# Grouping attention's matmuls by kind on TensorE, and layer norm in two bunches on VectorE

## The reference, cut to what matters

```python
h = _layernorm(x) * (1 + ca) + sa                       # modulation per sequence
x1 = _layernorm(h, ln1_g, ln1_b)
Q, K, V = low-rank projections of x1 (16 heads of 8)
scores = einsum('bhse,bhte->bhst', Q, K) / sqrt(8)      # causal mask
attn = softmax(scores, axis=-1)
ctx = einsum('bhst,bhtd->bhsd', attn, V)
h = h + ctx @ out_U @ out_V + out_b                     # then MLP, router, experts
```

## Time and profile before

| | |
|---|---|
| median of 3 runs | 906.88 us (906.5 to 907.08) |
| the profiled execution's own time | 905.57 us |
| its span, first to last instruction | 902.9 us |
| attention | from the start to about 447 us of the span |
| steady steps of attention | about 95 to 411 us |
| TensorE busy over the whole span | 672.0 us (74%) |
| VectorE, ScalarE, GpSimd busy | 419.0, 419.8, 312.9 us |

### The profile page before, as it was taken

One profiled execution on the slowest core, in us unless ns is written; L12 is line 12 of the kernel. 1 busy time (PEld: TensorE's weight loads), 2 busy tenths in 40 slices (PEclk: granted clock), 3 DMA queues, 4 the chain that ended last, 5 costly groups with the idle time before them and its releaser, 6 DMA issues. The chain is left out here.

```text
span 902.9 us, 15792 instructions
## 1 busy us (share of the span) xinstructions
PE 672.0 (74%) x5322; PEld 407.9 (45%) x5322; DVE 419.0 (46%) x1079; ACT 419.8 (46%) x733; POOL 312.9 (35%) x491
## 2 busy tenths in 40 slices
PE   4447999989899999998178885753328799999900
PEld 3213334433334433432146554433026699899900
DVE  1568887777775666661148763800003011111117
ACT  5120666656666665558255654311012355555513
POOL 2441323323332222121134432277730154455523
PEclk9999999999999999999679996985559799999965
DMA  8233323333333333112294111011100677778627
GB/s 178 83 111 128 110 81 127 99 111 106 122 100 125 105 124 106 47 48 76 67 271 92 46 47 61 30 55 51 51 27 0 184 226 215 223 208 227 187 87 207
DMA packets 104347, 102.68 MB, mean 114 GB/s; under 512 B 12912, under 2 KB 88600, under 8 KB 104192
## 3 DMA queue, kind: packets, MB, share of 16 engines
q1 hardware_dynamic: 95264, 89.12, 33.4%
q0 software_dynamic: 4544, 9.45, 3.0%
q10 hardware_dynamic: 4480, 3.35, 1.5%
HBM read 58.97 MB, written 38.72 MB: 108 GB/s over the span
## 5 line engine op out<-in xcount | busy, mean ns | idle before, releaser
L962 DVE TENSOR_REDUCE row_max<-ps_s 128x1 f32<-128x384 f32 (+3 forms) x384 | 216.2, 596 | 98.9 <-PE ps_s L722 75.8
L583 ACT ACTIVATE work<-ps_s 128x1024 f32<-128x1024 f32 (+1 forms) x192 | 168.5, 883 | 67.2 <-PE ps_s L751 64.7
L722 PE MATMUL ps_s<-k_st,q_st 128*128 128x384 bf16 (+3 forms) x512 | 129.2, 309 | 0.0
L1531 POOL DMA_INDIRECT y_d<-res,target x78 | 74.9, 960 | 124.5 <-DVE res L1596 109.5
L719 PE MATMUL ps_s<-later_q,ident_b 128*128 128x128 bf16 (+1 forms) x384 | 94.4, 250 | 17.2 <-DVE row_max L962 13.8
L768 PE MATMUL ps_pv<-work,v_sb 128*32 128x512 f32 (+3 forms) x1024 | 95.5, 446 | 1.3 <-ACT ctx_raw L617 1.2
L719 PEld LDWEIGHTS ps_s<-later_q,ident_b 128*128 128x128 bf16 x384 | 37.2, 98 | 113.2 <-DVE row_max L962 78.9
L1596 DVE TENSOR_TENSOR res<-ps_s,bias 128x256 f32<-128x256 f32 x39 | 16.6, 425 | 137.1 <-PE ps_s L1583 134.2
L1583 PEld LDWEIGHTS ps_s<-w_tile,x_hidden 128*128 128x128 f32 x624 | 75.6, 192 | 2.0
L1573 PE MATMUL ps_s<-tok_t,w_tile 128*128 128x256 f32 x312 | 76.2, 388 | 0.0
L1583 PE MATMUL ps_s<-w_tile,x_hidden 128*128 128x128 f32 x624 | 75.8, 275 | 0.0
(11 more groups left out here) (198 smaller groups left out, 1028.4 us busy)
## 6 DMA issues: line engine op xcount, KB each, us to landing
w_tile<-in_ew SPq DMA_DIRECT2D x39, 514.0 KB
ctx_d<-ctx_raw SPq DMA_DIRECT2D x32, 256.0 KB, 3.0
q_st<-q_d SPq DMA_DIRECT2D x64, 102.0 KB
k_st<-k_d SPq DMA_DIRECT2D x64, 96.0 KB
slots_d<-fill SPq DMA_DIRECT2D x1, 5148.0 KB, 23.1
rows<-slots_d SPq DMA_DIRECT2D x39, 132.0 KB
got<-y_d SPq DMA_DIRECT2D x16, 256.0 KB, 3.2
q_d<-qk_part SPq DMA_DIRECT2D x8, 384.0 KB, 2.7
```

Source lines behind the costliest of these rows:

```text
L583: act.activation(dst, src, ACT.Exp, scale=SCALE).then_inc(exp_done, 1)
L722: mm = pe.matmul(bnk[:, k * keys:(k + 1) * keys], q_st[b % 2][:, g, j, i * P:(i + 1) * P], k_st[b % 2][:, g, j // 2, 0:keys], start=False, ...
L962: dve.reduce_max(row_max[:, m % 2, js[0] % 2, j:j + len(js), i], src, AXIS.X).then_inc(max_taken, 1)
L1531: pool.indirect_dma_start(y_d[:], bass.IndirectOffsetOnAxis(ap=target[:, k, c:c + 1], axis=0), res[:, k, c, :], None).then_inc(put[k], 16)
```

## The change

On TensorE the order within a step changes, with the same matmuls. Before:

s2(0), ctx0, s1(0,1), s2(1), ctx1, [O], s1(2,3), M, s2(2), ctx2, [T] [K] [V], s1(4,5), s2(3), ctx3, s1(6,7), [Q], s2(4), s1(8,9), s2(5), s1(10,11).

After:

s2(0), s2(1), ctx0, s1(0,1), [O], s1(2,3), M, s2(2), s2(3), ctx1, ctx2, ctx3, s1(4,5), [T] [K] [V], s1(6,7), [Q], s2(4), s2(5), s1(8,9,10,11).

On ScalarE the exponential of piece 3 and the emptying of the product bank follow piece 2 directly. On VectorE the layer norm's instructions are issued in two bunches, after the maxima of pieces 3 and 7.

```diff
 # ScalarE
                         if has:
                             exp_unit(n, 2)
+                            exp_unit(n, 3)
+                        if 0 <= n - 1 < NG:
+                            empty_ctx(n - 1)
                         if batch_at(n, T_AT) is not None:
                             empty_t(batch_at(n, T_AT))
...
-                        if has:
-                            exp_unit(n, 3)
                         if batch_at(n, Q_AT) is not None:
                             empty_qk(batch_at(n, Q_AT), 0)
                         if has:
                             exp_unit(n, 4)
-                        if 0 <= n - 1 < NG:
-                            empty_ctx(n - 1)
-                        if has:
                             exp_unit(n, 5)
 # TensorE
                         s2(n, 0)
+                        s2(n, 1)
                         context(n - 1, 0)
                         s1(m, 0, 1)
-                        s2(n, 1)
-                        context(n - 1, 1)
                         if batch_at(n, OUT_AT) is not None:
                             project_out(batch_at(n, OUT_AT))
                         s1(m, 2, 3)
                         if 0 <= m - 1 < NG:
                             transpose_max(m - 1)
                         s2(n, 2)
-                        context(n - 1, 2)
+                        s2(n, 3)
+                        for kt in range(1, NT):
+                            context(n - 1, kt)
+                        s1(m, 4, 5)
                         if batch_at(n, T_AT) is not None:
...
-                        s1(m, 4, 5)
-                        s2(n, 3)
-                        context(n - 1, 3)
                         s1(m, 6, 7)
                         if batch_at(n, Q_AT) is not None:
                             project(batch_at(n, Q_AT), 0)
                         s2(n, 4)
-                        s1(m, 8, 9)
                         s2(n, 5)
-                        s1(m, 10, 11)
+                        s1(m, 8, 9, 10, 11)
 # VectorE
                     def layer_norm(n, u):
-                        i, second = divmod(u, 2)
+                        second = u == 7
                         b = batch_at(n, STATS_AT)
-                        if b is not None and b >= NORM_EARLY and i < NT:
-                            if second:
-                                moments_of(0, b, i, x_stats, x_moments)
-                            else:
-                                stats_x(b, i)
+                        if b is not None and b >= NORM_EARLY:
+                            for i in range(NT):
+                                if second:
+                                    moments_of(0, b, i, x_stats, x_moments)
+                                else:
+                                    stats_x(b, i)
...
                         b = batch_at(n, NORM_AT)
-                        if b is not None and b >= NORM_EARLY and i < NT and second:
-                            normalise(b, i)
+                        if b is not None and b >= NORM_EARLY:
+                            for i in (2, 3) if second else (0, 1):
+                                normalise(b, i)
...
-                            layer_norm(n, u)
+                            if u in (3, 7):
+                                layer_norm(n, u)
```

More of the change, by code:

```diff
@@ L939, in layer_norm @@
[L939 to L943, removed]
-                        b = batch_at(n, H_STATS_AT)
[L945 to L949, removed]
+                        if b is not None and b >= NORM_EARLY:
[4 more added lines that the diff above has]
+                                    stats_x(b, i)
@@ new lines, in layer_norm @@
+                        b = batch_at(n, SCALE_AT)
+                        if b is not None and b >= NORM_EARLY:
+                            for i in range(NT):
+                                if second:
+                                    shift_x(b, i)
+                                else:
+                                    scale_x(b, i)
+                        b = batch_at(n, H_STATS_AT)
+                        if b is not None and b >= NORM_EARLY:
+                            for i in range(NT):
+                                if second:
+                                    moments_of(1, b, i, h_stats, h_moments)
+                                else:
+                                    stats_h(b, i)
```

## The result

The changed kernel takes 909.25 us (median of 20 runs, 906.42 to 911.74), the kernel before 905.52 us in the same comparison (20 runs, 900.91 to 907.55). The ratio is 1.0044, 95% interval 1.0029 to 1.0058: **slower, by 3.7 us**, where +6 was forecast. The predicted 912.5 is 3.3 above, and the range of 902 to 921 holds the time. The profiled execution has a span of 905.5 us (before: 902.9).

A forecast was written before the change was run, and what follows sets the result against it. TensorE sets the pace, waiting on VectorE's row maxima through two banks. Attention +7.5 us, with the end starting 1.6 earlier, sums to +6 us: 912.9 for the median, stated as 912.5, range 902 to 921.

The forecast's parts named there:

- Which way, and why: Whole kernel: slower by what two banks between TensorE and VectorE cost, 908.7 to 917 us; chance 0.48.
- The saving of 0.90: TensorE, steady step: array shape changes 8 times instead of 16, saving 0.90 us a step.
- the lost cover of 1.69: First-score runs (pieces 0-3, 4-7, 8-11): bank waits 2.35 us a step in the new order, 0.66 in the old.
- the case called even: Whole kernel: same balance, off by 0.1 to 0.25 us a step, 905.1 to 908.7 us; chance 0.14.
- Drains win: TensorE: shape changes cost more than starts show; faster if above 0.14 us each, 898 us at 0.17; chance 0.19.
- Two s2 pieces in a row pay: Between paired s2 pieces: 0.10 us at three places in 32 steps, 9.6 us, giving 922; chance 0.07.
- The clock falls more often: TensorE: half clock once more in every group, 9 us, giving 921; chance 0.12.
- T, K, V in the second run: Between pieces 5 and 6: V adds only 0.13 us, K 0.12, and T fits into the wait.
- Layer norm's bunch after piece 7: VectorE: four shifts hold piece 8's maximum, lengthening the third run by 0.85 us once in four steps.
- Groups 0 to 3: First four steps: +1.2 us, with no O yet to cover the first run.
- Step 28: Late attention step 28: +0.4 us.
- The end: Step 31's first matmul to last copy: 8.5 us instead of 10.09; the DMA chain behind it starts 1.6 earlier.

The follow-up runs named there:

- the split third run: Changed kernel with s2(5) put back between first-score pieces 9 and 10: 900.57 us, ratio 0.9964 to the kernel before.
- Short maxima: Maxima read only each head's first 64 columns (work left out): changed kernel 866.37 us, ratio 0.9586; kernel before 875.54 us, 0.9694.
- the order alone: Changed kernel's TensorE and ScalarE order with layer norm spread as in the kernel before: 913.67 us, ratio 1.0098.
- the first covered order: Changed kernel with s2(1), products 2 and 3, or s2(5) moved between first-score pieces where other work leaves waits uncovered: 893.65 us, 0.9880; repeated, 891.77 us, 0.9874.
- the fastest: Mixed order with layer norm's second bunch after piece 5, M before O, O behind s2(2,3), s2(1) always between pieces 1 and 2: 879.67 us, 0.9753.

## Why the prediction was right, point by point

**Which way, and why: right.** The changes of shape save what they should: outside the three runs the quiet step takes 10.19 - 5.71 = 4.48 us, and the forecast's terms make 4.50. The runs take 1.68, 1.83 and 2.20, 5.71 together, of which the prediction had 3.34 as stream: 2.37 of waits for 2.35. The saving of 0.90 and the lost cover of 1.69 are both there, and the split third run shows the mechanism alone. Short maxima turn the sign, as they should if the waits are what the new order loses by. The size is less sure than the sign: the time lies only 0.5 us above the case called even, and the two profiled executions differ in more than the change, as said below.

**Drains win: refuted.** With maxima at their length the kernel isn't faster; at 0.12 for the mean of the two changes measured singly (0.09 and 0.145) the price is under the turning point of 0.14. The 0.10 by which V is slower behind products was missing, and it is why this rival came nearer than I had it. The Trainium skill, "TensorEngine Tiling (Array Packing)", section "Key Properties", says that a change of tiling mode drains the engine; the 0.33 agrees in that such changes cost time. The 29 us that the prediction worked out from that rule alone is still the wrong size: the 0.90 a step are saved, and the 1.69 of lost cover outweigh them.

**Two s2 pieces in a row pay: refuted,** 0.29 apart. **The clock falls more often:** not in this kernel's profiled execution (one half-clock stretch in its steady steps, two before). In the order alone three falls cost 4.5 us, against one of 1.0 here, and that is under half of the 7.7 us by which its steady steps are longer (316.24 and 308.59 us from M of step 0 to M of step 28); so 0.12 was no idle chance. How often it falls in the executions behind the medians no trace shows.

**The terms that were mis-sized**: most were forecast too large, step 28 and the end too favourably.

- T, K, V in the second run: V adds 0.05, not 0.13 (10.24 - 10.19), K nothing, not 0.12. I gave them the 0.97 that they take behind a product; among full-array pieces V takes 0.90 and K 0.86. A group costs +0.6 for +0.8.
- Layer norm's bunch after piece 7: 10.95 - 10.24 = 0.71, not 0.85. That it is about even with the 0.96 of the old kernel was right; that the same spread instructions would cost 46.52 - 44.22 = 2.3 a group on the new order the prediction didn't weigh.
- Groups 0 to 3: +1.1 with what precedes them, for +1.2. The 1.3 us won in steps 8 to 12 are the profile of before, not the change. In it these steps took 2.1 us more than steps 4 to 8: 1.2 after M of step 8, where 185 to 188 us stood at 0.50, and 0.87 after M of step 10, where VectorE waited for a DMA ahead of a reciprocal and the maxima of pieces 10 and 11 came late:

```profile
213.02 0.55 DVE L984 RECIPROCAL recs<-sums 128x64 f32<-128x64 f32 x1 [1.11 <-DMA sums<-ctx_d]
```

  Neither stands there now; without them the profiled pair would differ by 2.1 us more, nearer to the forecast. Up to M of step 28 it is +3.2 where the forecast's terms make +7.1, and half of that gap is this one group.
- Step 28, up to M of step 29: +1.25, not +0.4. That M waits 0.75 for GpSimd's last split of the maxima, which the forecast gave no wait. No first scores stand before M any more, and of the products only ctx0; in the old order ctx1 stood there too:

```profile
415.76 0.24 PE L727 MATMUL ps_m<-ident_b,neg_part 128*48 128x128 bf16 x1 [0.75 <-POOL neg_part L525]
```

- The end: from step 31's first matmul to the last copy 8.97, forecast 8.5, before 10.09:

```profile
425.74 0.21 PE L745 MATMUL ps_s<-ident_h,lower_k 64*128 64x64 bf16 x2 [1.06 <-ACT work L583]
...
434.71 0.60 ACT L617 ACTIVATE ctx_raw<-ps_pv 128x512 f32<-128x512 f32 x1 [2.60 <-PE ps_pv L766]
```

A gain of 1.1 for the 1.6 forecast. Attention ends 3.9 later for 6. What gives back 1.3 of that between the last copy and the end of the span wasn't traced.

## What to carry to other kernels

Read TensorE's wait for a bank as two numbers, the idle time of the engine and that of its weight load, and ask of every piece of other work whether it stands inside such a wait: there it is free, with its changes of array shape, and a denser order takes it out. Count the handoff (piece, way to the other engine, its work, release) against what stands between piece u and u+2, before putting a run of four on two banks. Look also at what GpSimd runs beside a VectorE instruction that stands ahead of a maximum. Save changes of shape only where no wait covers them; and where two uses share a bank, put the short one with the late follower first.

## What the runs showed of the hardware that I had not expected

**A bunch on VectorE beside GpSimd.** Two normalisations take 0.59 us in a row, but 2.49 in step 11 (1.27 and 1.30, each ending 0.08 to 0.09 after one of GpSimd's). VectorE's timeline, and GpSimd's of the same time:

```profile
216.82 0.59 DVE L854 TENSOR_SCALAR xn<-h_sb,moments,rstd 128x128 f32<-128x128 f32 x2
...
220.41 2.49 DVE L854 TENSOR_SCALAR xn<-h_sb,moments,rstd 128x128 f32<-128x128 f32 x2
```

```profile
220.32 1.27 POOL L542 TENSOR_TENSOR ctx_n<-ctx_t,rec_rows 128x512 f32<-128x512 f32 x1 [4.99 <-DMA rec_rows<-rec_d]
221.55 1.26 POOL L555 TENSOR_TENSOR h_sb<-h_sb,out_bias 128x512 f32<-128x512 f32 x1
```

Piece 10 then waited 1.21 for its maximum, and the interval is 14.31 instead of 13.61. With the bunch after piece 5 it began before GpSimd's pair in step 11 and took 0.59, but in step 7 it met GpSimd's instructions and took 2.39:

```profile
173.58 2.39 DVE L854 TENSOR_SCALAR xn<-h_sb,moments,rstd 128x128 f32<-128x128 f32 x2
```

Where they meet isn't fixed even for one kernel: the bunch of step 7 took 2.19 us in one profiled execution of the first covered order and 0.59 in the other. The Trainium skill, "SBUF — State Buffer", section "SBUF: two separate sides", describes the port pair that these two engines share as a lock held for a whole instruction, which fully blocks the other engine; for VectorE it names instructions in a 2-port mode or with two inputs in SBUF. The trace agrees in kind, with VectorE's two instructions ending 0.08 to 0.09 after GpSimd's of 1.27 and 1.26; in which mode they ran no run shows.

**A float32 matmul group right behind 32-column tiles took longer**: 0.99 us instead of 0.89 for V, besides the change of shape before it. Why, no run shows.

**The half clock comes and goes, for one and the same kernel too.** Steady steps show one or two stretches at half clock (the kernels after and before), three (the order alone) and none (the fastest). But the first covered order, profiled twice, shows none in one execution and two in the other, so one profile doesn't tell what an order does to the clock. The fastest, from M of step 0 to M of step 28:

```profile
98.07:379.10 281.03, 272.25 (x2942) 122.44 (x2942) 210.95 (x460) 191.64 (x270) 86.78 (x193) 1.00 0.33 111
```

In the profiled steady steps each fall to 1.2 GHz came within 3 us after TensorE had idled for 1.0 to 1.9 us, mostly at M after the output projection; the fastest kernel idles at most 0.65 us at a time there and shows no fall. But other such waits, most of M's in the changed kernel among them, brought none, so what tells the one from the other stays open.
